# One operand of VectorE's scaling and one-hot build moved to PSUM, and four sum banks instead of eight, in a seven-layer graph network kernel

## The reference

```python
def gat_conv(x, src, dst, W, a_src, a_dst, b):          # block 0, twice
    ...
    alpha = ex / (s[dst] + 1e-16)
    out = segment_sum(h[src] * alpha[:, :, None], dst, num_segments=N)   # 4 heads x 64

def _graph_conv(x, src, dst, W_rel, b, W_root):         # block 1, three times
    agg = segment_sum(x[src], dst, num_segments=N)
    return agg @ W_rel + b + x @ W_root

msgs = edge_vals[:, None] * x[edge_src]                 # block 2, once
agg = segment_sum(msgs, edge_dst, num_segments=N)

a = ex / denom[dst] * dist                              # block 3, once
m = ft[src] * a
out = segment_sum(m, dst, num_segments=n)
```

## Time and profile before

| | us |
|---|---|
| median of 3 runs | 12187.51 |
| lowest, highest | 12166.11, 12193.12 |
| the profiled execution's own time | 12139.19 |
| its span, first to last instruction | 12137.7 |

### The profile page before, as it was taken

The page is one execution under the profiler, slowest core; times in us unless marked ns, Lnnn a source line. Parts: engine busy times, 40 slices in busy tenths (PEclk is TensorE's granted clock), DMA queues, the critical chain, the costliest instruction groups (busy, mean ns, idle before and its releaser), DMA issues. The chain is left out here.

```text
span 12137.7 us, 120576 instructions
## 1 busy us (share of the span) xinstructions
PE 6937.7 (57%) x25379; PEld 4270.1 (35%) x25380; DVE 6291.8 (52%) x11430; ACT 691.5 (6%) x2515; POOL 7475.9 (62%) x6875
## 2 busy tenths in 40 slices
PE   1994544498545525556555565555545567965553
PEld 1443333343333312224322242233433344433332
DVE  5556555555655563344433343344655565555556
ACT  0001000100000000001100020000100012000000
POOL 0337777534777766665666646665577732357775
PEclk8556777655777756667766676667777775556776
DMA  2542333553233343333333333333333335533334
GB/s 90 131 111 75 87 88 88 135 121 104 74 88 87 87 107 88 90 88 91 90 89 87 88 92 88 89 89 87 104 88 88 88 78 154 121 83 87 88 88 101
DMA packets 574611, 1153.38 MB, mean 95 GB/s; under 512 B 141672, under 2 KB 335002, under 8 KB 573645
## 3 DMA queue, kind: packets, MB, share of 16 engines
q0 software_dynamic: 314480, 807.51, 25.1%
q1 hardware_dynamic: 253577, 338.53, 10.2%
q10 hardware_dynamic: 6480, 6.55, 0.2%
HBM read 1080.25 MB, written 78.23 MB: 95 GB/s over the span
## 5 line engine op out<-in xcount | busy, mean ns | idle before, releaser
L681 POOL DMA_INDIRECT l0bg_messages<-table_h,l0bg_index x832 | 1026.0, 1233 | 279.9 <-issue 253.0
L681 POOL DMA_INDIRECT l0ag_messages<-table_h,l0ag_index x832 | 1023.3, 1230 | 279.8 <-issue 253.0
L681 POOL DMA_INDIRECT l3g_messages<-table_h,l3g_index x832 | 1018.3, 1224 | 279.1 <-issue 253.0
L681 POOL DMA_INDIRECT l2a_messages<-table,l2a_index x832 | 985.4, 1184 | 291.2 <-issue 253.3
L681 POOL DMA_INDIRECT l1aa_messages<-table,l1aa_index x832 | 835.1, 1004 | 438.2 <-issue 248.4
L681 POOL DMA_INDIRECT l1ba_messages<-table,l1ba_index x832 | 833.2, 1001 | 409.1 <-issue 250.4
L681 POOL DMA_INDIRECT l1ca_messages<-table,l1ca_index x832 | 833.0, 1001 | 403.5 <-issue 246.1
L815 PE MATMUL l1aa_sums<-l1aa_messages,l1aa_member 128*128 128x256 f32 x1664 | 662.1, 532 | 724.4 <-issue 328.0
L815 PE MATMUL l2a_sums<-l2a_messages,l2a_member 128*128 128x257 f32 x1664 | 617.0, 549 | 672.9 <-DVE l_acc L779 567.1
L815 PE MATMUL l1ba_sums<-l1ba_messages,l1ba_member 128*128 128x256 f32 x1664 | 653.0, 524 | 607.0 <-issue 294.5
L815 PE MATMUL l1ca_sums<-l1ca_messages,l1ca_member 128*128 128x256 f32 x1664 | 660.2, 530 | 593.9 <-issue 316.1
(11 more groups left out here) (522 smaller groups left out, 12590.3 us busy)
## 6 DMA issues: line engine op xcount, KB each, us to landing
l0al_src_codes<-codes_dram SPq DMA_DIRECT2D x104, 384.0 KB
l0bl_src_codes<-codes_dram SPq DMA_DIRECT2D x104, 384.0 KB
l3l_src_codes<-codes_dram SPq DMA_DIRECT2D x104, 384.0 KB
l0al_dst_codes<-codes_dram SPq DMA_DIRECT2D x104, 256.0 KB
l0bl_dst_codes<-codes_dram SPq DMA_DIRECT2D x104, 256.0 KB
l3l_dst_codes<-codes_dram SPq DMA_DIRECT2D x104, 256.0 KB
l0ag_messages<-table_h,l0ag_index POOLq DMA_INDIRECT x832
l0bg_messages<-table_h,l0bg_index POOLq DMA_INDIRECT x832
```

Source lines behind the costliest of these rows:

```text
L681: pool.indirect_dma_start(out=self.messages[:, s, j, 0:D], out_offset=None, in_=table, in_offset=bass.IndirectOffsetOnAxis(ap=self.index[: ...
```

## The change

1. Each `aggregate_phase` allocates four sum banks (`SUMS = 4`) instead of eight. Chunk j uses bank j % 4, and its matmul waits for the add of the chunk four before it, in units' second halves also in the very first unit.
2. A bank `operands` holds a copy of `k.iota` (128 columns, made once per phase) and the current unit's scales (8 columns, or 32 in the attention layers).
3. `begin` reads `iota` from that bank. Its other input stays in SBUF.
4. `take` in the scaled layers first waits for the scaling of the unit before (`prepared`), copies the unit's scales to the bank, waits for the gathers and for the copy (`scale_here`), and multiplies with the scales from PSUM. In the plain layers it waits for the gathers as before.

```diff
+SUMS = 4
...
-        sums = [m.ps(f"sums{j}", [P, 512]) for j in range(U)]
+        sums = [m.ps(f"sums{j}", [P, 512]) for j in range(SUMS)]
+        wide = H if head_scale else 1
+        operands = m.ps("operands", [P, 512])
+        iota_ps = operands[:, 0:P]
+        scale_ps = operands[:, P:P + U * wide]
+        iota_made, scale_here = m.sem("iota_made"), m.sem("scale_here")
...
-                dve.tensor_tensor(member[:, s % 2], repeat_outer(k.iota[:], U),
+                dve.tensor_tensor(member[:, s % 2], repeat_outer(iota_ps, U),
                                   repeat_inner(k.local[:, bass.ds(u * U, U)], P), ALU.is_equal).then_inc(member_made, 1)
 
             def take(i, s):
-                dve.wait_ge(gathered[s], i * (16 * U) + 16 * U)
+                u = i * SLOTS + s
                 msgs = ring[:, s, :, 0:D]
-                if scale is None:
+                if scale is not None and not before(u, 1):
+                    dve.wait_ge(prepared, u)
+                if head_scale:
+                    dve.tensor_copy(scale_ps.rearrange("p (c h) -> p c h", h=H),
+                                    by_chunk(scale)[:, bass.ds(u * U, U), :]).then_inc(scale_here, 1)
+                    dve.wait_ge(gathered[s], i * (16 * U) + 16 * U)
+                    dve.wait_ge(scale_here, u + 1)
+                    heads = msgs.rearrange("p j (h f) -> p j h f", h=H)
+                    weights = scale_ps.rearrange("p (c h) -> p c h", h=H).unsqueeze(3).to_broadcast([P, U, H, C])
+                    dve.tensor_tensor(heads, heads, weights, ALU.mult).then_inc(prepared, 1)
+                elif scale is not None:
+                    dve.tensor_copy(scale_ps, scale[:, bass.ds(u * U, U)]).then_inc(scale_here, 1)
+                    dve.wait_ge(gathered[s], i * (16 * U) + 16 * U)
+                    dve.wait_ge(scale_here, u + 1)
+                    dve.tensor_tensor(msgs, msgs, repeat_inner(scale_ps, D), ALU.mult).then_inc(prepared, 1)
+                else:
+                    dve.wait_ge(gathered[s], i * (16 * U) + 16 * U)
                     dve.sem_inc(prepared, 1)
...
-                    dve.tensor_tensor(at, at, sums[j][:, 0:width], ALU.add).then_inc(chunk_added, 1)
+                    dve.tensor_tensor(at, at, sums[j % SUMS][:, 0:width], ALU.add).then_inc(chunk_added, 1)
...
             dve.memset(ring[:, :, :, MSG_ONE], 1.0).then_inc(set_up, 1)
+            dve.tensor_copy(iota_ps, k.iota[:]).then_inc(iota_made, 1)
+            dve.wait_ge(iota_made, 1)
...
-                    if not first:
-
-                        pe.wait_ge(chunk_added, u * U + (j + 2 - U))
-                    pe.matmul(sums[j][:, 0:width], member[:, s % 2, j, :], ring[:, s, j, 0:width],
+                    if not first or j >= SUMS:
+                        pe.wait_ge(chunk_added, u * U + (j + 2 - SUMS))
+                    pe.matmul(sums[j % SUMS][:, 0:width], member[:, s % 2, j, :], ring[:, s, j, 0:width],
                               start=True, stop=True).then_inc(chunk_summed, 1)
```

More of the change, by code:

```diff
@@ L748, in begin @@
                 dve.wait_ge(index_ready, u + 1)
-                dve.tensor_tensor(member[:, s % 2], repeat_outer(k.iota[:], U),
+                dve.tensor_tensor(member[:, s % 2], repeat_outer(iota_ps, U),
                                   repeat_inner(k.local[:, bass.ds(u * U, U)], P), ALU.is_equal).then_inc(member_made, 1)
             def take(i, s):
-                dve.wait_ge(gathered[s], i * (16 * U) + 16 * U)
+                u = i * SLOTS + s
                 msgs = ring[:, s, :, 0:D]
-                if scale is None:
-                    dve.sem_inc(prepared, 1)
[L758 to L766, removed]
+                if scale is not None and not before(u, 1):
+                    dve.wait_ge(prepared, u)
```

## The result

| | kernel before | changed kernel |
|---|---|---|
| median, us | 12187.10 | 12624.43 |
| lowest, highest | 12166.11, 12193.12 | 12605.08, 12645.01 |
| runs | 4 | 4 |

The ratio is 1.0362 (95% interval 1.0349 to 1.0374): 437 us slower, where -24 us were forecast and the range ended at 12,430.

What follows compares the result with a forecast made beforehand. GpSimd was taken to bound the scaled layers, VectorE's held-up queue the plain ones. Scaled layers -27 us and iota copies +3, other terms 0, gave -24 us from 12,187.51: 12,163 us, range 11,900 to 12,430.

Steps and rivals of the forecast that it cites:

- GpSimd's stops: Gathers beside scaling and one-hot build: all should take 0.95 us, 2.0 us less a unit in l0b, 1.9 in l2.
- Length of the moved operations, copies: VectorE's build and scaling from PSUM: no added length, 0; copies covered by gather waits, except seven of iota, 3 us.
- The second bound: VectorE's queue, held up when gathers follow each other without long stops: a pace of some 11.9 to 12.0 us a unit.
- full gain: Rival: only plain layers have the hold-up, scaled layers run at GpSimd's 10.0 us a unit; -798 us, 11,390; chance 0.13.
- What is late next: Scaled layers l0a, l0b, l2, l3: they fall only to the plain layers' pace, 11.96 us a unit; -27 us.
- Four banks: Sum banks of the aggregations: no stall of the adds, and later release of ring slots covered; 0.
- The plain layers: l1a, l1b, l1c: builds stop no gather, but GpSimd does not hold these layers, so 0 us.
- The second rival: Scaled layers: VectorE's held queue costs more, late slot release helping; 12.6 us a unit, +242 us, 12,430; chance 0.28.

Runs made afterwards that it cites:

- chip B: Three chips of the follow-up runs that agree within 0.1%; the kernel before, unchanged, takes 11,762 to 11,766 us there.
- chip A: Chip number 4 of the follow-up runs; the kernel before, unchanged, takes 12,135 us there, the changed kernel 12,554.02 us.
- the pause that might have helped: Changed kernel plus a GpSimd memset of 1600 columns after each unit's eight gathers: 11,730.71 us, ratio 0.9972, on chip B.

## Why the prediction was wrong

*GpSimd's stops.* Right. Gathers beside a VectorE instruction with one input in PSUM take 945 ns in the layers shown, on both chips. By the Trainium skill (SBUF — State Buffer, "Who interferes with whom"), as the prediction read it, the two operations could not have stopped a gather; the runs on chip B, 472 us for iota and 517 for the scales, speak against that inference for these gathers.

*Length of the moved operations, copies.* Right: 2288 ns for 2292, builds at 1218 to 1220, copies of 0.20 us.

*The second bound.* Right in kind, and its price was right for seven banks: "a pace of some 11.9 to 12.0 us a unit" was measured as 11.91 to 12.11 on chip A. But it was taken for a property of the kernel. On chip B it does not show, and the rival "full gain" came out there, with -941 us for the -798 worked out; the plain layers gained too (l1b 10.82, with both operands in SBUF, to 10.15), which had been booked with 0.

*What is late next.* Nearly right as it stands. The scaled layers were given the plain layers' pace of before, 11.96 us, and with seven banks on chip A they took 12.00 (l0b) and 12.11 (l2). The whole kernel had 60 us more there, not 24 less.

*Four banks.* This is the step that failed: the term was put at 0, and the runs on chip A show 359 us between seven banks and four with unstopped gathers. In the sum the slot's release came 2.3 + 4 x 0.63 = 4.8 us after the landing, with adds 0.63 us apart. But the same sum expected the scaled layers to be held up as the plain ones are, and there adds stand 2.8 us apart; in the timeline above four adds took 8.1 us instead of 2.5. "When VectorE is behind, it is not covered" was left to a rival, though the sum itself had VectorE held up. On chip A this is no exception: 47 of the 104 units of l0b and 35 of l1b have a pause of GpSimd of over 0.5 us. With stopped gathers the term is small (42 us), so 317 us of the 419 belong to the two edits together, and neither line of the sum could hold them.

*The plain layers.* Wrong for the same reason: 0 was taken, they lost 0.50 us a unit in l1b. With seven banks on chip A l1b is at 11.91, as with stopped gathers (11.92).

*The second rival* had the right sign and the right place, and named the shorter ring; its 12,430 us was too little by 194. That it came as near is in part luck, for it was priced from a row that was misread. Of the 709.2 us before the adds of l1b, 404.0 "issue", I called all above l0b's a hold-up, 5.4 us a unit. On chip B the same group shows 573.0 us with 399.7 "issue" and no hold-up (no two adds of a unit are over 1.04 us apart): in a plain layer the wait for a unit's gathers has no instruction of its own, and stands before its first add. What does show a hold-up is the spacing of adds inside a unit, 2.8 us for 0.62.

*Open.* What holds VectorE's queue up on chip A, and why chip B has none, is not known. Chip A is one group of runs on one chip, so the chip itself and whatever else went on around it at that time are not told apart. A kernel's profiled time agrees with its other runs within 0.4%, on both chips, so nothing here tells whether the recording takes a part. Why four banks cost more there is argued from the longer pauses and from one timeline, not shown: the runs that would have parted the late release from the turns over four banks, and the pause that might have helped, never ran on chip A. The timeline speaks for the late release, since its adds did not wait for TensorE. TensorE's clock may take a part too: from 3310 to 3318 us there, where it did one product of 1.25 us in every 2.1 to 3.4 us, its granted clock was 0.50, the lower of its two levels (1.2 GHz), and it was 0.649 over the changed kernel's span against 0.689 with seven banks; no run separates it.

## What to carry to other kernels

Two edits that each take slack from the same ring must be costed together, and with the delays that the rest of the sum assumes: one made the gathers denser, the other held their slots longer, and on the chip where that mattered +60 and +42 us became +419. If an operand needs a PSUM bank of its own, give up one bank and not four: in this kernel seven sum banks are as good on chip B (10,827 us for 10,821) and lose 0.5% instead of 3.4% on chip A. A verdict from one chip is a verdict on that chip, so run the pair on a second one before a few per cent are trusted.

## What the runs showed of the hardware

- A VectorE tensor_tensor with both inputs in SBUF (fp32, 1024 or 2048 elements per partition) lengthens the gather that GpSimd issues beside it, from 0.95 us to 1.8 or 2.3; with one of the inputs in PSUM it does not, and takes as long itself (1218 and 2288 ns). Together the two moved operands are worth 8.4% of the kernel with four banks on chip B (11,810 to 10,821 us).
- Chips of one kind ran the same kernel 3.2% apart (12,135 us on one, 11,762 to 11,766 on three), with most of it in the plain layers: l1b of one kernel 11.92 against 10.82 us a unit, l0b 11.89 against 11.88. On chip A VectorE's adds come 2 to 5 us apart in stretches; in the traces of four banks alone, seven banks and the changed kernel on chip B, no add of a unit starts more than 1.04 us after its neighbour.
- Half the bytes per gather changed GpSimd's time for one from 947 to 944 ns (l1b, seven banks, chip B).
